# The LSTM's input products of two steps as seven block products, with partial sums taken out of PSUM by VectorE

## The chip, the cores and the metric

The kernel runs on one core of one Trainium2 chip. The metric is the device time of one execution in microseconds (us). The kernel before takes 1242.64 us, the median of three runs (1242.17 to 1243.83).

## The reference: what is computed

An LSTM over 128 time steps and then a GRU over the same 128 steps, for 32 sequences, with 512 features and a state of 512. Each layer's output is added to its input.

```python
# LSTM (Wx, Wh: 512 x 2048), h0 = cond_1024, c0 = 0
a = x[:, t] @ Wx + b + prev_h @ Wh
i, f, o = sigmoid(a[:, :512]), sigmoid(a[:, 512:1024]), sigmoid(a[:, 1024:1536])
g = tanh(a[:, 1536:])
c = f * c + i * g ;  h = o * tanh(c)
y = x + h                                   # input of the GRU
# GRU (each of W*, U*: 512 x 512), its state s starts at 0; video = cond_1024
z  = sigmoid(y[:, t] @ W_z + s @ U_z + vz)  # vz = video @ C_z + b_z, and so on
r  = sigmoid(y[:, t] @ W_r + s @ U_r + vr)
hh = tanh(y[:, t] @ W + (r * s) @ U + vh)
s  = (1 - z) * s + z * hh
out = y + s
```

## The kernel before

**Tiles.** The four chunks of 32 columns of a gate lie on four groups of 32 partitions. So every product is issued as four matmuls, one for each j, each with a stationary operand of 128 x 32 (32 sequences of one chunk of 128 features) and a moving one of weights; the four write four partition groups of one PSUM bank and run beside each other. I call four such matmuls a set.

**Precision.** Each fp32 operand is split into a high and a low fp16 part, and a product is three passes: high by high, high by low, low by high (PASSES). With four chunks of features (K) that is 12 sets for a product over all features. The scales of the split come from the largest |x| of a group of four steps (largest, bound, lstm_scales, gru_scales). The first steps (t < FL = 4 for the LSTM, t < F = 8 for the GRU) use fp32 matmuls on the weights as given, while the weights are split.

**A tick.** `ticks` runs t from 0 to 128. In tick t the LSTM does step t and the GRU step s = t - 1. Each engine has its own program, in order, and semaphores join them; the order is written by hand. q = t % 4 is the place in the group, r the half of the double buffers. On TensorE a tick from t = 9 on is:

- the product of `wh` with the LSTM's state, 512 columns, 12 sets (waits `h_hi`, `h_lo`), in bank `ps_l[t % 4]`; with it the gates of step t are complete
- the product of `w` with y, 384 columns (three gates), 12 sets (waits `y_hi`, `y_lo`, and `cand_sum`), in `ps_g`
- the product of `u` with the GRU's state, 256 columns (z and r), 12 sets (waits `g_hi`, `g_lo`); `zr_ps` tells VectorE
- the product of `wx` with x of step t + 1, 512 columns, 12 sets, in bank `ps_l[(t+1) % 4]` (waits `ifo_sum` of three steps ago); once in each group `bound` follows
- the product of `u` with r * s, 128 columns, 12 sets (waits `rg_hi`, `rg_lo`); `cand_ps` tells VectorE

**VectorE in a tick:** the gates' sums out of PSUM (`undone`: times a scale, plus a bias), `ig_fc`, the cell, the sum for z and r, then the new state (`new_state`), `rg`, its transpose and its parts, the low part of h, `keep`, the work of the group (`turn`, `lstm_scales`, `turn_out`, the low part of x, `gru_scales`, `largest`), the candidate's sum, `zc`, `g_nat`, its transpose and its low part. ScalarE does the sigmoids, tanhs and the high parts; GpSimd (POOL) adds x and h into yT, scales it, makes the low part of y, and adds up the output. SP issues the loads of x and the stores.

**Lines.** L780 is the matmul of `product`, L541 is `undone`, L538 `lo_part`, L346 ScalarE's `hi_part`, L889 the wait ahead of the product with `w`, L928 the wait for `x_lo` ahead of the product with `wx`, L822 `bound`.

Of the kernel before, what the change touches and what calls it, by code (L numbers as in the profile page):

```python
# [5 lines left out]
def lstm_then_gru(nc, x, cond, wx, wh, b0, w_z, u_z, c_z, b_z, w_r, u_r, c_r, b_r, w_h, u_h, c_h, b_h, out):  # L6
# [8 lines left out]
    B, T, D = x.shape  # L15
# [34 lines left out]
    with ExitStack() as ctx:  # L50
# [75 lines left out]
        ps_c = psum("ps_c", [P, GL * P])  # L126
        ps_squares = ps_c[:, GG * P:GG * P + 2 * K + 2 * GG]
# [23 lines left out]
        cond_ps = sem("cond_ps")  # L151

# [81 lines left out]

        @block.sync
        def _(sp):
# [28 lines left out]
            def tick(t, n, i):  # L265
                q, r = n % Q, n // Q
                group = 2 * i + r
                if q == 0 and (group + 2 < NG):

                    sp.wait_ge(xT_done, group + 1)  # L270
                    load(t + 2 * Q, r)
                if t >= 2 * Q + 1 and t % Q == (1 if t < T else 0):
                    store(Q * (group - 2), r, group - 2)
# [7 lines left out]
        def _(pool):  # L281
# [24 lines left out]
            def tick(t, n, i):  # L306
# [28 lines left out]
        def _(act):  # L335
# [107 lines left out]
            def tick(t, n, i):  # L443
# [25 lines left out]
                if (q == 1 and 0 < group < NG - 1) or t == 2:  # L469
# [16 lines left out]
                after_cand(t)  # L486

# [3 lines left out]
        def _(dve):  # L491
# [51 lines left out]
            def lstm_scales(r, group):  # L543
# [4 lines left out]
                nc.vector.tensor_scalar(t0, ps_bound[:, r:r + 1], 1.0, None, ALU.add).then_inc(base_done, 1)  # L548
# [72 lines left out]
            def after_keep(t):  # L621
# [12 lines left out]
                if t == T_WU_SCALE + 4:  # L634
                    u_low(1, 1)

            def after_cand(t):
# [39 lines left out]
            def tick(t, n, i):  # L677
# [7 lines left out]
                if lstm:  # L685
                    if q == 0:
                        dve.wait_ge(scl_done, group + 1)
                    dve.wait_ge(gates_ps, t + 1)
                    undone(gates[:, 3 * P:4 * P], ps_l[t % NL][:, 3 * P:4 * P], r_l(r), term0[:, 3, :]).then_inc(tg_sum, 1)
                    undone(ifo, ps_l[t % NL][:, 0:3 * P], r_l(r), term0[:, 0:3, :].rearrange("p g c -> p (g c)")  # L690
                           ).then_inc(ifo_sum, 1)
# [41 lines left out]
                if q == 0 and 0 < group < NG - 1:  # L733
# [4 lines left out]
                if t >= 2 * Q + 1 and t % Q == (1 if t < T else 0):  # L738
                    dve.wait_ge(out_done[r], 16 * J * i)
                    turn_out(r, group - 2)  # L740
                if q == 2 and (group + 1 < NG):
                    dve.wait_ge(x_hi, group + 1)
                    lo_part(x2T[:, 1 - r, LO, :], xT[:, 1 - r, :], a_x(1 - r), x2T[:, 1 - r, HI, :]).then_inc(x_lo, 1)
# [3 lines left out]
                if q == 3 and (group + 2 < NG):  # L747
                    dve.wait_ge(x_in[r], 16 * J * (i + 2))
                    largest(r)
                if gru:  # L750
# [3 lines left out]
                    after_cand(t)  # L754
                    dve.wait_ge(cand_done, s + 1)
# [7 lines left out]
                    nc.vector.transpose(gT[:, s % 2, :], g_nat[:]).then_inc(gT_done, 1)  # L763
                    if F - 1 <= s < T - 1:
# [9 lines left out]
        def _(pe):  # L774
# [26 lines left out]
            def w_of(b, k, j):  # L801
                return w12[:, b, k, :, :].rearrange("p g (n j c) -> p j (g n) c", j=J, c=B)[:, j]
# [13 lines left out]
            HALF, WAIT = 6, 8  # L816
# [12 lines left out]
            def gate_as_given(bank, g, still, raw_weights, chunks, opens, closes):  # L829
# [3 lines left out]
                return mm  # L833

# [10 lines left out]
            def tick(t, n, i):  # L845
# [15 lines left out]
                elif lstm:  # L861
                    if t == FL:
                        pe.wait_ge(wh_split, HALVES * K)
                    pe.wait_ge(h_hi, t + 1 - FL)
# [21 lines left out]
                elif F <= m < T:  # L886
# [3 lines left out]
                    product(ps_g[m % 2], 0, GG * P, w_of, y_of(m % Q), 0, HALF, True, False)  # L890
# [31 lines left out]
                if FL - 1 <= t < T - 1:  # L922
# [7 lines left out]
                if q == 0 and 0 < group < NG - 1:  # L930
                    bound(1 - r, group + 1)
                if recurs and s < F:
# [40 lines left out]
```

## Time and profile before

| | |
|---|---|
| time, median of 3 runs | 1242.64 us (1242.17 to 1243.83) |
| the profiled execution's own time | 1244.18 us |
| its span | 1242.4 us |
| mean granted clock of TensorE | 0.989 of full speed |
| TensorE matmuls busy | 1205.5 us, 97% of the span |
| TensorE weight loads busy | 763.8 us, 61% |
| VectorE busy | 872.4 us, 70% |
| ScalarE busy | 445.0 us, 36% |
| GpSimd busy | 278.0 us, 22% |

PE is TensorE's matmuls and PEld its weight loads, which run beside them; DVE is VectorE, ACT ScalarE, POOL GpSimd. Times of the trace are counted from the start of the span. A row of matmuls shows when its first began and for how long the row ran; its end is modelled and overlaps the next row, so a block of sets is measured from its start to the start of the next.

### The profile page before, as it was taken

What the parts mean: (1) busy time and instruction counts of PE and PEld (TensorE: products, weight loads), DVE (VectorE), ACT (ScalarE), POOL (GpSimd) and SP (SyncE); (2) the same over time, 40 slices, a digit from 0 to 9 for tenths busy, and PEclk for the clock granted to TensorE, in tenths of its full rate; (3) what the DMA queues carried; (4) which work ended last, traced back from release to release, by engine and by line L of the source; (5) the groups of instructions that cost most, each with busy time, mean ns of one, the idle gap of its engine ahead of it and who ended that gap; (6) DMA issues with size and microseconds to landing.
All of it is one profiled execution on the core that took longest, in us unless ns stands there. A gap on an engine that the chain in (4) does not pass through costs nothing.

```text
span 1242.4 us, 67987 instructions
## 1 busy us (share of the span) xinstructions
PE 1205.5 (97%) x31013; PEld 763.8 (61%) x31013; DVE 872.4 (70%) x2681; ACT 445.0 (36%) x1078; POOL 278.0 (22%) x520
## 2 busy tenths in 40 slices
PE   5889999999999999999999999999999999999996
PEld 1457666666666666666666666666666666666664
DVE  2568877777777777777776777777777777677765
ACT  5555233333333333333333333333333333333332
POOL 3100222222212222222222221222222222222221
PEclk9899999999999999999999999999999999999998
DMA  9900100111110111110011111011111001110001
GB/s 304 317 9 12 20 10 14 21 20 20 21 19 6 20 21 21 20 21 12 12 21 21 20 21 20 5 19 20 21 21 21 13 11 21 20 20 12 12 8 24
DMA packets 142000, 39.50 MB, mean 32 GB/s; under 512 B 135760, under 2 KB 136016, under 8 KB 140688
## 3 DMA queue, kind: packets, MB, share of 16 engines
q1 hardware_dynamic: 140016, 34.49, 12.9%
q8 instruction: 243, 3.98, 1.3%
q0 software_dynamic: 640, 0.53, 0.2%
q14 instruction: 45, 0.37, 0.1%
q10 hardware_dynamic: 1056, 0.13, 0.1%
HBM read 26.74 MB, written 8.39 MB: 28 GB/s over the span
## 4 chain that ended last, share of the span: by engine, by line
PE 93%; SPq 3%; DVE 2%; DMA 1%; issue 1%; ACT 0%; POOLq 0%; POOL 0%; DVEq 0%
PE ps_l L780 51%; PE ps_g L780 38%; PE ps_g L789 3%; SPq L239 2%; DMA o_area<-in_L_cond_C_dram 1%; PE ps_l L789 1%; SPq L243 1%; PE ps_bound L822 0%; DVE wh L538 0%; DVE u L538 0%; DVE zr L541 0%; SPq L248 0%; SPq L250 0%; PE ps_c L789 0%; ACT zr L457 0%
## 5 line engine op out<-in xcount | busy, mean ns | idle before, releaser
L780 PE MATMUL ps_l<-wh,h2T 128*32 128x512 f16 x5952 | 344.4, 380 | 3.3 <-DVE wh L538 3.3
L780 PE MATMUL ps_l<-wx,x2T 128*32 128x512 f16 x5952 | 342.8, 379 | 0.0
L780 PE MATMUL ps_g<-w,y2T 128*32 128x384 f16 x5760 | 256.2, 327 | 0.0
L780 PEld LDWEIGHTS ps_l<-wx,x2T 128*32 128x32 f16 x5952 | 160.6, 97 | 134.2
L780 PEld LDWEIGHTS ps_l<-wh,h2T 128*32 128x32 f16 x5952 | 154.6, 97 | 138.7 <-DVE wh L538 3.6
L780 PEld LDWEIGHTS ps_g<-w,y2T 128*32 128x32 f16 x5760 | 155.3, 97 | 92.3
L320 POOL TENSOR_TENSOR yT<-xT,hT 128x128 f32<-128x128 f32 x128 | 61.9, 484 | 589.8 <-DVE hT L670 589.8
L780 PE MATMUL ps_g<-u,g2T 128*32 128x256 f16 x5760 | 178.5, 273 | 0.8 <-ACT g2T L485 0.8
L780 PEld LDWEIGHTS ps_g<-u,g2T 128*32 128x32 f16 x5760 | 154.7, 97 | 16.9 <-issue 1.2
L541 DVE SCALAR_TENSOR_TENSOR zr<-ps_g,sc,term 128x256 f32<-128x256 f32 x128 | 61.9, 484 | 108.0 <-PE ps_g L780 100.5
L304 POOL TENSOR_TENSOR o_area<-yT,gT 128x128 f32<-128x128 f32 x128 | 58.6, 458 | 307.3 <-DVE gT L763 307.3
L541 DVE SCALAR_TENSOR_TENSOR gates<-ps_l,sc,term 128x128 f32<-128x128 f32 (+1 forms) x256 | 111.4, 476 | 13.7 <-PE ps_l L789 6.3
L696 DVE TENSOR_TENSOR ig_fc<-gates,tg_cell 128x256 f32<-128x256 f32 x128 | 54.4, 425 | 76.5 <-ACT gates L450 76.4
L780 PE MATMUL ps_g<-u,rg2T 128*32 128x128 f16 x5760 | 101.9, 220 | 4.4 <-DVE rg2T L535 4.4
L780 PEld LDWEIGHTS ps_g<-u,rg2T 128*32 128x32 f16 x5760 | 90.2, 97 | 25.2 <-DVE rg2T L535 4.6
L457 ACT ACTIVATE zr<-zr 128x256 f32<-128x256 f32 x128 | 53.3, 416 | 134.8 <-DVE zr L541 134.7
L479 ACT ACTIVATE cand<-cand 128x128 f32<-128x128 f32 x128 | 39.6, 309 | 155.3 <-DVE cand L541 155.3
L485 ACT ACTIVATE g2T<-gT,sc 128x128 f16<-128x128 f32 x120 | 48.3, 402 | 125.9 <-DVE gT L763 125.9
L538 DVE SCALAR_TENSOR_TENSOR g2T<-gT,sc,g2T 128x128 f16<-128x128 f32 x120 | 42.1, 351 | 58.5 <-ACT g2T L485 58.5
L328 POOL TENSOR_TENSOR y2T<-y_scaled,y2T 128x128 f16<-128x128 f32 x120 | 68.7, 573 | 49.6 <-ACT y2T L468 49.6
L325 POOL TENSOR_SCALAR y_scaled<-yT,sc 128x128 f32<-128x128 f32 x120 | 77.1, 643 | 11.8
L448 ACT ACTIVATE tg_cell<-gates 128x128 f32<-128x128 f32 x128 | 39.6, 310 | 107.0 <-DVE gates L541 107.0
(101 smaller groups left out, 1107.3 us busy)
## 6 DMA issues: line engine op xcount, KB each, us to landing
out_dram<-o_area SPq DMA_DIRECT2D x128, 64.0 KB, 2.1
x_nat<-in_x_dram SPq DMA_DIRECT2D x126, 64.0 KB, 2.7
wh<-in_L_cond_Wx_dram SPq DMA_DIRECT2D x4, 1024.0 KB, 12.0
w<-in_L_cond_Wh_dram SPq DMA_DIRECT2D x3, 1024.0 KB, 20.4
u<-in_L_cond_Wh_dram SPq DMA_DIRECT2D x1, 1024.0 KB, 26.5
stage<-in_L_cond_W_z_dram SPq DMA_DIRECT2D x1, 1024.0 KB, 8.5
stage<-in_L_cond_W_r_dram SPq DMA_DIRECT2D x1, 1024.0 KB, 8.1
stage<-in_L_cond_W_dram SPq DMA_DIRECT2D x1, 1024.0 KB, 10.3
```

What stands on the lines that cost most here:

```text
L304: nc.gpsimd.tensor_tensor(oT[:, r, q, :], yT[:, q, :], gT[:, m % 2, :], ALU.add).then_inc(oT_done, 1)
L320: nc.gpsimd.tensor_tensor(yT[:, q, :], xT[:, r, P * q:P * q + P], hT[:, n % 2, :], ALU.add).then_inc(yT_done, 1)
L325: nc.gpsimd.tensor_scalar(y_scaled[:, n % 2, :], yT[:, q, :], a_y(r), None, ALU.mult).then_inc(y_scaled_done, 1)
L328: nc.gpsimd.tensor_tensor(y2T[:, q, LO, :], y_scaled[:, n % 2, :], y2T[:, q, HI, :], ALU.subtract).then_inc(y_lo, 1)
L448: nc.scalar.activation(tg_cell[:, 0:P], gates[:, 3 * P:4 * P], ACT.Tanh)
L457: nc.scalar.activation(zr[:], zr[:], ACT.Sigmoid).then_inc(zr_done, 1)
L485: nc.scalar.mul(g2T[:, HI, :], gT[:, s % 2, :], a_g(m_next // Q)).then_inc(g_hi, 1)
L538: return nc.vector.scalar_tensor_tensor(lo, value, scale, hi, ALU.mult, ALU.subtract)
L541: return nc.vector.scalar_tensor_tensor(to, ps, scale, term, ALU.mult, ALU.add)
L696: nc.vector.tensor_tensor(ig_fc[:], gates[:, 0:2 * P], tg_cell[:], ALU.mult).then_inc(ig_fc_done, 1)
L780: mm = nc.tensor.matmul(bank[B * j:B * j + B, c0:c1].rearrange("p (n c) -> p n c", c=B), still(a, k), moving(b, k, j), start=opens and (a, ...
L789: mm = nc.tensor.matmul(bank[rows(j), c0:c0 + weights.shape[1] // J].rearrange("p (n c) -> p n c", c=B), still[:, B * chunk:B * chunk + B] ...
```

## The change

For a pair of steps u, u + 1 (u even, u >= FW = 24) the input products are a product of a matrix of 2 by 2 blocks (two steps by two halves of the features) with one of 2 by 2 blocks (two halves of the features by two halves of the 2048 columns). They are made from seven products of blocks instead of eight, with sums of blocks of x (S1 to S4) and of blocks of Wx (T1 to T4). One block product is 6 sets (three passes, two chunks) of 256 columns. Four partial sums for each pair leave PSUM through VectorE into `pre`, in place of the bias, and the gates' sums then add `pre` instead of `term0`. The rest:

- Wx is loaded again at t = 9; GpSimd makes T1 to T4 at t = 11 to 14 (two subtractions of 128 x 1024 in each), ScalarE splits one at the end of ticks 12, 13, 15 and 16, VectorE makes the low parts in ticks 13, 14, 16 and 17, two instructions of 128 x 1024 in each. GpSimd makes S1 to S4 once for each group at q = 3 (128 x 128 each); they are split once for each group (128 x 512).
- From t = 9 on (m >= F) the product of `w` is in two: 256 columns (z and r) at its old place, and 128 columns (the candidate's) just before the product with r * s, behind a wait for `zr_sum`.
- The work of a group stands elsewhere: `turn_out` and the store at q = 3 of the next group; for groups from the sixth on `largest` at q = 2, `turn` at q = 3, the scales at q = 0 and x's parts at q = 0 and 1, most of them right behind the gates' sums on VectorE.

```diff
@@ VectorE
+            def first_out(u):
+                evict(1, u, pre[:, u % NL, H1], ps_l[(u + 1) % NL][:, H2], bias0(H1))
+            def fifth_out(u):
+                evict(2, u, pre[:, (u + 1) % NL, H2], ps_fifth[:, H1], bias0(H2))
+            def sixth_out(u):
+                dve.wait_ge(evicted, 2 * (u - FW) + 2)
+                evict(3, u, pre[:, u % NL, H2], ps_l[(u + 1) % NL][:, H2], pre[:, (u + 1) % NL, H2])
+            def seventh_out(u):
+                evict(4, u, pre[:, (u + 1) % NL, H1], ps_l[(u + 1) % NL][:, H2], bias0(H1))
...
+                if q == 0 and NG_W <= group + 1 < NG:
+                    lstm_scales(1 - r, group + 1)
...
+                if FW <= t < T and q % 2 == 0:
+                    seventh_out(t)
...
+                    if FW <= t + 2 < T and q % 2 == 0:
+                        first_out(t + 2)
+                    if FW <= t + 1 < T and q % 2 == 1:
+                        sixth_out(t + 1)
...
+                    if FW <= t + 2 < T and q % 2 == 0:
+                        fifth_out(t + 2)
@@ TensorE
+                    if t >= FW and q % 2 == 1:
+                        pe.wait_ge(evicted, 2 * (t - FW) + 2)
                     pe.wait_ge(h_hi, t + 1 - FL)
...
-                    product(ps_g[m % 2], 0, GG * P, w_of, y_of(m % Q), 0, HALF, True, False)
+                    product(ps_g[m % 2], 0, 2 * P, w_of(0, 2), y_of(m % Q), 0, WAIT, True, False)
+                    pe.wait_ge(y_lo, m + 1 - F)
+                    product(ps_g[m % 2], 0, 2 * P, w_of(0, 2), y_of(m % Q), WAIT, END, False, False)
...
-                if FL - 1 <= t < T - 1:
+                if FL - 1 <= t < FW - 1:
...
+                if q % 2 == 0:
+                    if FW <= t < T:
+                        pe.wait_ge(evicted, 2 * (t - FW) + 3)
+                        seventh(ps_l[(t + 1) % NL], 1, s_of(r, 3, q // 2), t_of(N_T3), False).then_inc(seven_ps, 1)
+                    if FW <= t + 2 < T:
...
+                        pe.wait_ge(ifo_sum, v - NL + 1)
+                        seventh(ps_l[v % NL], 0, a_of(ru, qu + 1, 1), t_of(N_T4), True)
+                        seventh(ps_l[v % NL], 1, a_of(ru, qu, 0), b_of(0, 0), False).then_inc(seven_ps, 1)
...
+                        seventh(ps_fifth, 0, s_of(ru, 1, qu // 2), t_of(N_T1), True).then_inc(seven_ps, 1)
+                elif FW <= t + 1 < T:
...
+                    pe.wait_ge(evicted, 2 * (u - FW) + 1)
+                    seventh(ps_l[v % NL], 1, s_of(ru, 2, qu // 2), t_of(N_T2), False).then_inc(seven_ps, 1)
+                    pe.wait_ge(ifo_sum, u - NL + 1)
+                    seventh(ps_l[u % NL], 0, a_of(ru, qu, 1), b_of(1, 0), True)
+                    seventh(ps_l[u % NL], 1, s_of(ru, 4, qu // 2), b_of(1, 1), False)
...
+                if F <= m < T:
+                    pe.wait_ge(zr_sum, m + 1)
+                    product(ps_g[m % 2], 2 * P, 3 * P, w_of(2, 3), y_of(m % Q), 0, END, False, False)
@@ GpSimd and ScalarE
+                if t == T_MADE:
+                    pool.wait_ge(again_in, 16 * K)
+                    make_t(t1, b12, b11)
...
+                if T_MADE + 1 <= t <= T_MADE + 2:
+                    split_high(t - T_MADE - 1)
```

TensorE, two ticks in the middle of the kernel before (`product` is L780; `x48` is 12 sets):

```order
L780 MATMUL ps_l<-wh,h2T 32x512 x48
L780 MATMUL ps_g<-w,y2T 32x384 x48
L780 MATMUL ps_g<-u,g2T 32x256 x48
L780 MATMUL ps_l<-wx,x2T 32x512 x48
L780 MATMUL ps_g<-u,rg2T 32x128 x48
L780 MATMUL ps_l<-wh,h2T 32x512 x48
L780 MATMUL ps_g<-w,y2T 32x384 x48
```

The same engine now, an even tick from its product with `u` on, and the odd one behind it (L963 is `product`, L1023 the block product `seventh`, `stage` holds the T, the S and `pre`, `ps_c` is the fifth partial sum's bank):

```order
L963 MATMUL ps_g<-u,g2T 32x256 x48
L1023 MATMUL ps_l<-stage 32x256 x24
L1023 MATMUL ps_l<-stage,x2T 32x256 x24
L1023 MATMUL ps_l<-wx,x2T 32x256 x24
L1023 MATMUL ps_c<-stage 32x256 x24
L963 MATMUL ps_g<-w,y2T 32x128 x48
L963 MATMUL ps_g<-u,rg2T 32x128 x48
L963 MATMUL ps_l<-wh,h2T 32x512 x48
L963 MATMUL ps_g<-w,y2T 32x256 x48
L963 MATMUL ps_g<-u,g2T 32x256 x48
L1023 MATMUL ps_l<-stage 32x256 x24
L1023 MATMUL ps_l<-wx,x2T 32x256 x24
```

(One more block product of the odd tick follows.) The product of `wx` with 512 columns became four block products in the even tick and three in the odd one, and the candidate's part of the product with `w` moved behind them.

VectorE in a tick with q = 2 of the kernel before, from the keep on:

```order
L730 SCALAR_TENSOR_TENSOR keep<-zr,g_nat 128x128
L538 SCALAR_TENSOR_TENSOR x2T<-xT,sc,x2T 128x512
L558 TENSOR_SCALAR sc<-factors,base 128x2
L559 TENSOR_SCALAR sc<-undo,base 128x1
L541 SCALAR_TENSOR_TENSOR cand<-ps_g,sc,term 128x128
L756 TENSOR_TENSOR zc<-zr,cand 128x128
L759 TENSOR_TENSOR g_nat<-zc,keep 128x128
L763 STREAM_TRANSPOSE gT<-g_nat 128x128
L538 SCALAR_TENSOR_TENSOR g2T<-gT,sc,g2T 128x128
```

The same stretch now (L654 is `undone`, L651 `lo_part`):

```order
L900 SCALAR_TENSOR_TENSOR keep<-zr,g_nat 128x128
L654 SCALAR_TENSOR_TENSOR stage<-ps_l,sc,term 128x256
L675 TENSOR_SCALAR sc<-factors,base 128x2
L676 TENSOR_SCALAR sc<-undo,base 128x1
L654 SCALAR_TENSOR_TENSOR cand<-ps_g,sc,term 128x128
L654 SCALAR_TENSOR_TENSOR stage<-ps_l,sc,term 128x256
L937 TENSOR_TENSOR zc<-zr,cand 128x128
L940 TENSOR_TENSOR g_nat<-zc,keep 128x128
L944 STREAM_TRANSPOSE gT<-g_nat 128x128
L654 SCALAR_TENSOR_TENSOR stage<-ps_c,sc,term 128x256
L651 SCALAR_TENSOR_TENSOR g2T<-gT,sc,g2T 128x128
```

Three partial sums stand in an even tick: ahead of the candidate's sum, behind it, and behind the transpose of g. The odd tick has one, behind the candidate's sum. The low part of x moved to the front of the tick before.

## Rows read from the trace of the kernel before

**Rows 1.** Busy us (x instructions) of PE, PEld, DVE, ACT, POOL; PEclk; DMA.

```profile
300.00:400.00 100.00, 100.00 (x2631) 63.47 (x2627) 71.85 (x227) 33.33 (x89) 23.54 (x44) 1.00 0.08 14
1200.00:1243.00 43.00, 31.32 (x824) 20.57 (x811) 23.80 (x71) 9.95 (x27) 6.92 (x15) 0.86 0.13 21
```

**Rows 2.** Timeline, one tick: start us, us, engine, line, op.

```profile
600.92 2.76 PE L780 MATMUL ps_l<-wx,x2T 128*32 128x512 f16 x48
601.15 0.48 DVE L541 SCALAR_TENSOR_TENSOR zr<-ps_g,sc,term 128x256 f32<-128x256 f32 x1 [0.69 <-PE ps_g L780]
...
603.12 0.35 DVE L538 SCALAR_TENSOR_TENSOR rg2T<-rgT,sc,rg2T 128x128 f16<-128x128 f32 x1
...
603.51 0.84 PE L780 MATMUL ps_g<-u,rg2T 128*32 128x128 f16 x48
...
603.85 0.68 DVE L562 TENSOR_REDUCE raw<-x_nat 128x1 bf16<-128x512 f32 x1
603.88 0.43 POOL L328 TENSOR_TENSOR y2T<-y_scaled,y2T 128x128 f16<-128x128 f32 x1 [0.41 <-ACT y2T L468]
...
604.18 2.76 PE L780 MATMUL ps_l<-wh,h2T 128*32 128x512 f16 x48
604.44 0.34 DVE L541 SCALAR_TENSOR_TENSOR cand<-ps_g,sc,term 128x128 f32<-128x128 f32 x1
...
605.16 0.29 DVE L756 TENSOR_TENSOR zc<-zr,cand 128x128 f32<-128x128 f32 x1 [0.38 <-ACT cand L479]
...
606.16 0.40 ACT L485 ACTIVATE g2T<-gT,sc 128x128 f16<-128x128 f32 x1 [1.03 <-DVE gT L763]
...
606.60 0.35 DVE L538 SCALAR_TENSOR_TENSOR g2T<-gT,sc,g2T 128x128 f16<-128x128 f32 x1 [0.47 <-ACT g2T L485]
606.77 2.12 PE L780 MATMUL ps_g<-w,y2T 128*32 128x384 f16 x48
607.06 0.88 DVE L541 SCALAR_TENSOR_TENSOR gates<-ps_l,sc,term 128x128 f32<-128x128 f32 x2
...
608.53 0.42 DVE L696 TENSOR_TENSOR ig_fc<-gates,tg_cell 128x256 f32<-128x256 f32 x1 [0.59 <-ACT gates L450]
...
608.72 1.48 PE L780 MATMUL ps_g<-u,g2T 128*32 128x256 f16 x48
...
610.03 2.76 PE L780 MATMUL ps_l<-wx,x2T 128*32 128x512 f16 x48
```

**Rows 3.** Groups by shape, 300 to 1200 us: busy us, mean ns, idle before.

```profile
L541 DVE SCALAR_TENSOR_TENSOR zr<-ps_g,sc,term 128x256 f32<-128x256 f32 x98 | 47.4, 484 | 80.7 <-PE ps_g L780 80.7
L304 POOL TENSOR_TENSOR o_area<-yT,gT 128x128 f32<-128x128 f32 x98 | 44.9, 458 | 203.7 <-DVE gT L763 203.7
L538 DVE SCALAR_TENSOR_TENSOR x2T<-xT,sc,x2T 128x512 f16<-128x512 f32 x25 | 18.6, 745 | 0.0
L474 ACT ACTIVATE x2T<-xT,sc 128x512 f16<-128x512 f32 x24 | 17.2, 718 | 0.0
```

**Rows 4.** Groups by shape, 90 to 180 us, where W and U are split.

```profile
L538 DVE SCALAR_TENSOR_TENSOR w<-stage,cols,w 128x1024 f16<-128x1024 f32 x6 | 7.5, 1278 | 0.0
L346 ACT ACTIVATE u<-stage,cols 128x2048 f16<-128x2048 f32 x3 | 5.9, 1988 | 0.0
```

**Rows 5.** Timeline of PE around the last tick of that split.

```profile
140.88 1.49 PE L780 MATMUL ps_g<-u,g2T 128*32 128x256 f16 x48 [0.83 <-ACT g2T L485]
...
145.32 0.85 PE L780 MATMUL ps_g<-u,rg2T 128*32 128x128 f16 x48 [0.36 <-DVE rg2T L535]
```

**Rows 6.** Line L928, then L889: waits of PE's sequencer, first and last start.

```profile
L928 PEldq EVENT_SEMAPHORE  x1: 51/51/51, 600.2 to 600.2; - x1
L889 PEldq EVENT_SEMAPHORE  x1: 51/51/51, 605.3 to 605.3; - x1
```

**Rows 7.** Timeline of PE at the end.

```profile
1226.98 3.48 PE L780 MATMUL ps_g<-w,y2T 128*32 128x384 f16 x48
```

**Rows 8.** The page's DMA issues: KB each, median us to landing.

```profile
wh<-in_L_cond_Wx_dram SPq DMA_DIRECT2D x4, 1024.0 KB, 12.0
```

More of the change, by code:

```diff
@@ L151, in lstm_then_gru @@
         cond_ps = sem("cond_ps")
+        again_in = sem("again_in")
+        t_made = sem("t_made")
+        t_hi = sem("t_hi")
+        t_split = sem("t_split")
+        xs_done = sem("xs_done")
+        xs_hi = sem("xs_hi")
+        xs_lo = sem("xs_lo")
+        seven_ps = sem("seven_ps")
+        evicted = sem("evicted")
         raw_x = sem("raw_x")
@@ L271, in tick @@
                     load(t + 2 * Q, r)
-                if t >= 2 * Q + 1 and t % Q == (1 if t < T else 0):
-                    store(Q * (group - 2), r, group - 2)
+                if t == T_AGAIN:
+                    sp.wait_ge(cand_ps, F - 1)
+                    sp.wait_ge(w1_split, HALVES * GG)
+                    sp.wait_ge(u1_split, HALVES * GG)
+                    for k in range(K):
+                        sp.dma_start(wx_again[k], wx[P * k:P * k + P, :]).then_inc(again_in, 16)
+                if q == Q - 1 and group >= 1:
+                    store(Q * (group - 1), 1 - r, group - 1)
             ticks(tick)
@@ L296, in _ @@
                 pool.sem_inc(out_done[r], 16 * J)
+            pool_made = [0]
             def add_out(s, m, group):
@@ L468, in tick @@
                     nc.scalar.copy(y2T[:, q, HI, :], y_scaled[:, n % 2, :]).then_inc(y_hi, 1)
-                if (q == 1 and 0 < group < NG - 1) or t == 2:
+                if (q == 1 and 0 < group < NG_W - 1) or t == 2:
                     act.wait_ge(xT_done, group + 2)
@@ L732, in tick @@
                 after_keep(t)
-                if q == 0 and 0 < group < NG - 1:
+                if FW <= t < T and q % 2 == 0:
+                    seventh_out(t)
+                if q == 0 and 0 < group < NG_W - 1:
                     if t >= Q:
@@ L746, in tick @@
                         gru_scales(1 - r, group + 1)
-                if q == 3 and (group + 2 < NG):
+                if q == 3 and group + 2 < NG_W:
                     dve.wait_ge(x_in[r], 16 * J * (i + 2))
@@ L833, in gate_as_given, with seventh, a_of, s_of @@
                 return mm
+            def seventh(bank, half, operand, weights, opens):
+                for a, b in PASSES:
+                    for k in range(K // 2):
+                        for j in range(J):
+                            mm = nc.tensor.matmul(bank[rows(j), 2 * P * half:2 * P * half + 2 * P].rearrange("p (n c) -> p n c", c=B),
+                                                  operand(a, k),
+                                                  weights(b, k).rearrange("p (n j c) -> p j n c", j=J, c=B)[:, j],
+                                                  start=opens and (a, b, k) == (HI, HI, 0), stop=(a, b, k) == (LO, HI, K // 2 - 1),
+                                                  skip_group_check=True)
+                return mm
+            def a_of(r, q, half):
+                return lambda a, k: x2T[:, r, a, P * q + B * (2 * half + k):P * q + B * (2 * half + k) + B]
+            def s_of(r, n, m):
+                c = P * (n - 1) + P // 2 * m
+                return lambda a, k: xs2[:, r, a, c + B * k:c + B * k + B]
+            def b_of(half, columns):
+                return lambda b, k: wx2[:, b, 2 * half + k, N2 * columns:N2 * columns + N2]
+            def t_of(n):
+                return lambda b, k: t_parts[n][:, b, k, :]
             pe.wait_ge(zeroed, 3)
```

145 lines of the change are left out of this document (128 added, 17 removed).

## The prediction

> **What bounds the kernel now.** I read the busy time by stretch first [rows 1]. From 300 to 400 us, as in each stretch to 1200, TensorE is busy for 100.00 of 100 us at clock 1.00, VectorE for 72, ScalarE for 33, GpSimd for 24. Busy matmuls can still be stretched ones, so next I read the timeline of one tick by the starts of its blocks [rows 2]: `wx` 600.92 to 603.51 is 2.59 us for 12 sets of 512 columns, `u` with r * s to 604.18 is 0.67 (128 columns), `wh` to 606.77 is 2.59, `w` to 608.72 is 1.95 (384), `u` to 610.03 is 1.31 (256). The sum is 9.11 us, the next `wx` starts 9.11 us after the first, and no row of PE has an idle time. Per set this is 216, 56, 162 and 109 ns: each is its columns at 2.4 GHz (213, 53, 160, 107) and about 2.5 ns more. So TensorE's columns set the time. `bound` comes once in a group before and after, so it drops out.
>
> **TensorE's sum.** Before, a pair of ticks has two `wx` blocks, 5.18 us. Now it has seven block products of 6 sets of 256 columns, at the `u` block's 1.31 us for 12 sets: 7 x 0.655 = 4.585. That is 0.595 less. The product of `w` is now 1.31 + 0.67 = 1.98 instead of 1.95: 0.03 more in each tick. A pair gives back 0.595 - 0.06 = 0.535 us, and there are (128 - 24) / 2 = 52 pairs: **-27.8 us**. The 16 ticks from 9 to 24 and the last pay only the 0.03: **+0.5 us**.
>
> **Do the states still come in time?** I set Z as the start of the block behind `u`. The sum for z and r starts at Z + 0.23 and then VectorE runs without a pause to Z + 2.93, where `keep` has made room (603.85 less 600.92) [rows 2]. Now r * s goes in at Z + 2.62 + 0.67 = Z + 3.29 in an even tick and Z + 1.97 + 0.67 = Z + 2.64 in an odd one. Its high part is ready when its low part starts, Z + 2.20, its low part 0.35 later, needed 0.45 us into the block: 0.4 us to spare in the odd tick, over 1 in the even one. `wh` starts at Z + 3.96 or Z + 3.31.
>
> The four evictions have the shape of the sum for z and r, 484 ns, some 0.43 of VectorE's time each [rows 3]. They stand in its idle times. The seventh goes from Z + 2.93 to about Z + 3.4; the candidate's sum must wait for TensorE until about Z + 4.15 anyway, and `wh` of the odd tick, which waits for this eviction, starts at Z + 3.96: 0.5 us to spare. The first and the sixth lie between the candidate's sum and `zc`, which starts 0.72 us behind it because it waits 0.38 for ScalarE [rows 2]; 0.28 + 0.43 fill that exactly. The fifth lies before the low part of g, where VectorE waits 0.47. So g is ready 2.1 (high) to 2.5 us (low) behind the start of the candidate's sum, at Z + 6.3 and Z + 6.7, and `u` now asks for the high part 3.9 us behind the start of `wh`, at Z + 7.9 (even) or Z + 7.2 (odd, where the candidate's sum is 0.5 earlier too). Behind the gates' sums VectorE waits 0.59 for ScalarE; the 0.7 us moved there (the low part of x is 0.745) delays `ig_fc` by 0.1 to 0.3, and the sum for z and r starts 2.5 us behind the gates' sums, where `ig_fc` and the cell were done at 2.2. ScalarE has 1.4 us more at the end of the q = 0 tick (twice 0.718), 0.5 of it past the start of the next gates' tanh; that uses the 0.3 up and no more. y has 2.7 us before `w` asks for it (603.88 + 0.43 against 606.77 less the GpSimd's semaphore), and the four sums S take 4 x 0.458 in a queue that idles for three quarters. Cost of all this at steady state: **0**. If VectorE's cover were gone the price would be the overrun in each tick.
>
> **The T blocks, ticks 12 to 17.** VectorE gets two instructions of 1.28 us in each of four ticks, ScalarE one of 1.99 at the end of four [rows 4]. Followed: ScalarE ends its split 0.9 us late for tick 13's tanh, 1.8 late for tick 14's; r * s is late by some 0.5 there. In tick 14 VectorE has 2.56 and x's low part and scales ahead of g: g's high part about 1.5 late for `u`. Tick 16 (the turn of x and its scales) 1.3 late, tick 17 0.9 and 0.3. Sum 4.5 us. The same working for tick 8 of the kernel before, with three such instructions, gave 1.2 us where the row says 0.83 [rows 5], so I take it for a little high, and its range from 2 to 8: **+4.5 us**. Tick 9's two waits of before, 0.83 and 0.36: the first grows by the missing 0.65 and the 128 columns then cover the second: **+0.1**.
>
> GpSimd's subtractions of 128 x 1024 are not in the trace. From the nearest row, 458 ns for 128 columns [rows 3], they take 0.46 us (all of it fixed) to 3.7 (all by column). At 3.7 two in a tick and its own 2.1 us are 9.5 in a tick of 9.1, four times: 1.6 us late, against y's 2.7. I cost them at 0 at both ends; a slower rate than the row's would show in y. Wx again is four loads of 12.0 us each [rows 8], issued together when U is split, about when tick 9's `u` block starts (140.88) [rows 5], and wanted late in tick 11, over 20 us later: in time if they overlap as at the start.
>
> **The end.** At 1226.98 the clock has fallen (0.86 in the last stretch; the last `w` block's row is 3.48 us long, 2.12 in mid-kernel) [rows 1, 2, 7]. `w` of 256 columns is 0.65 shorter in tick 127 and about 1 in tick 128, and the candidate's columns run while TensorE waits for r * s: **-1.6 us**.
>
> **Sum** against the profiled execution (1244.18 us, span 1242.4): -27.8 + 0.5 + 4.5 + 0.1 - 1.6 = -24.3, so 1219.9. That execution is 1.5 above the median of the runs; from 1242.64 it gives 1218.3. I say **1219**.
>
> **Can TensorE be fed that fast?** A pair had 480 matmuls, each with its load, in 18.2 us: 38 ns for each of the two together. Now it has 648 in 17.7: 27 ns, and the 96 ahead of every `wh` run at 14. The trace shows how far the sequencer is ahead: it met the wait at L928 at 600.2, 0.7 us before the block behind it began at 600.92, and L889 at 605.3, 1.5 before 606.77 [rows 6]. At 27 and at 54 ns for a matmul both are some 26 matmuls, also behind 24 matmuls at 27 ns, so a pace of 27 does not drain it. The block of r * s took 48 in 0.67 us and `wh` followed without a gap: with 26 in store the supply is at most 26 ns for each. Now 96 and the first 4 behind them need 74 beyond the store in 1.34 us, 18 ns each. The rows allow anything from 0 to 26, and the cost goes from nothing up to 74 x 26 - 1340, near 0.6 us a tick, 70 us over 120 ticks. I take 0, since the nearest row (the block at 14 ns for each) shows no stretch at all.
>
> The Trainium skill has a rule against this change: "Runtime: NRT & Kernel Launch", section "Instruction fetch mechanics", names a floor of about 20 cycles for each instruction. The page's floor, as an estimate at the 1.2 GHz of the sequencer in "Advanced Engine Details and Errata", section "Clock Domains", is 33 ns for a matmul with its load, and the changed kernel would then be slower by some 1.9 us a tick. The trace disagrees: 48 matmuls with their loads at 27 ns each in the `u` block left the sequencer as far ahead as before [rows 2, 6].
>
> **Rivals.**
>
> 1. *The feeding binds* (the other side). Place: the 96 matmuls of 128 columns. It costs from 18 ns up, and cancels the gain of 24 us at 0.2 us a tick, a supply of 20.8 ns. At the middle of what then remains, 23.5 ns: 74 x 23.5 - 1340 = 0.40 us, 120 times 48: **1267 us**. For it: nothing in the trace ran 96 in a row at this pace. Against: the block of 48 is exact to the last set.
> 2. *VectorE becomes a part of the bound.* It gets 4 x 0.43 and a quarter of 0.745 twice for each pair, so from 6.6 us a tick to some 7.6 of 8.84, and each eviction fits by 0.1 or less in its idle time. If each tick lost 0.15 (reads of PSUM beside TensorE's writes, longer waits): 104 x 0.15 = 16: **1235 us**.
> 3. *The T phase is costlier*, VectorE, ScalarE and GpSimd pushing each other beyond the 8: +8 more, **1227 us**.
> 4. *The seven products don't run at the `u` block's pace* (their moving operand lies in `stage` and is read with another stride). At 5 ns more for a set, 42 x 5 = 0.2 us a pair: **1230 us**.
>
> **Chances.** The forecast 0.58 (its own range 1214 to 1224), rival 1 0.14, rival 2 0.13, rival 3 0.08, rival 4 0.07. The range leaves the upper part of rival 1 out and keeps the best case, no stall at T and the full sum: 1214 to 1245. 0.2% is 2.5 us, about what a measurement of this kernel can tell from no change. Faster than 1240.2: 0.58, nearly all of 2, 3 and 4, a little of 1: 0.83. Within: 0.05. Slower: 0.12.
>
> **What will show it.** In a tick after 220 us block products of 0.655 us from start to start and no idle row of PE; a pair of 17.7 us; `w` of 128 columns directly ahead of r * s, both at 0.67. Rival 1 shows as 12 sets of 128 columns that take more than 0.67 while every semaphore has long been there. Rival 2 shows as PE rows with an idle time from `evicted`, `rg2T` or `g2T`. The T phase shows PE idle between 170 and 220 us: 2 to 8 us in all. The prediction is wrong if PE idles at all in steady ticks, or if the pair is not 17.7.

## The result

The changed kernel takes 1309.44 us, the median of four runs (1307.51 to 1313.48), against 1242.45 for the kernel before beside it. The ratio is 1.054, with a 95% interval from 1.051 to 1.057: 67 us slower, where the forecast was 23 faster. TensorE's clock is no large part of that: the granted clock is 0.99 on the mean in both profiled executions, and 1.00 in mid-kernel. Between the start and the end of the kernel it falls only where T is made, as told below.

The stretches of the changed kernel, as [rows 1] of before (busy us of PE, PEld, DVE, ACT, POOL with the number of instructions; PEclk; DMA share; GB/s):

```profile
180.00:220.00 40.00, 31.08 (x868) 19.73 (x860) 33.68 (x68) 14.21 (x30) 21.24 (x18) 0.91 0.10 16
300.00:400.00 100.00, 94.64 (x3422) 81.77 (x3411) 79.62 (x240) 34.64 (x90) 26.79 (x51) 1.00 0.09 15
```

TensorE, which had no idle time in [rows 1], has 5 us in each 100 of the steady part, and 9 in the 40 around the making of T. The waits between 300 and 1200 us say what ended them (us in total, times, longest us):

```profile
PE ps_g L963 <- issue: 30.8, 39, 1.5
PE ps_l L963 <- issue: 14.7, 23, 1.3
PE ps_l L963 <- DVE stage L654: 2.7, 2, 1.5
PE ps_l L1023 <- issue: 1.0, 4, 0.3
```

"Issue" is time in which TensorE waited for no semaphore. The evictions (`stage L654`) end two of the waits. The timeline shows where such a stop stands, here over an even tick:

```profile
608.54 0.92 PE L1023 MATMUL ps_l<-stage 128*32 128x256 f16 x24
...
609.20 0.92 PE L1023 MATMUL ps_l<-stage,x2T 128*32 128x256 f16 x24
...
609.86 0.50 PE L1023 MATMUL ps_l<-wx,x2T 128*32 128x256 f16 x11
...
610.69 0.61 PE L1023 MATMUL ps_l<-wx,x2T 128*32 128x256 f16 x13 [0.34 <-issue]
...
611.04 0.93 PE L1023 MATMUL ps_c<-stage 128*32 128x256 f16 x24
...
611.69 0.88 PE L963 MATMUL ps_g<-w,y2T 128*32 128x128 f16 x47
...
612.42 0.77 PE L963 MATMUL ps_g<-u,rg2T 128*32 128x128 f16 x40
614.71 0.11 PEld L963 LDWEIGHTS ps_g<-u,rg2T 128*32 128x32 f16 x5 [1.70 <-issue]
614.71 0.29 PE L963 MATMUL ps_g<-u,rg2T 128*32 128x128 f16 x5 [1.52 <-issue]
614.81 2.31 PEld L963 LDWEIGHTS ps_l<-wh,h2T 128*32 128x32 f16 x48
614.84 2.77 PE L963 MATMUL ps_l<-wh,h2T 128*32 128x512 f16 x48
```

While it runs, a block product keeps its pace: 608.54 to 609.20 is 0.66 us. But work stops in the middle of a block, after 11 of 24 or after some 43 of 48 matmuls, with nothing to wait for, and weight loads stop with it. Between the stops stand:

```profile
602.45:610.65 8.20, 7.86 (x256) 6.38 (x255) 6.44 (x22) 2.67 (x7) 3.02 (x8) 1.00 0.28 44
610.65:614.65 4.00, 2.49 (x128) 2.30 (x128) 1.34 (x5) 0.30 (x1) 0.95 (x2) 1.00 0.01 4
```

Matmuls and loads together, 512 and then 256. I took all pauses over 260 ns between two starts of TensorE from 300 to 1200 us: 80, and each of the 79 distances between them is a multiple of 256 instructions within 4. The DMA queue that brings instructions agrees in its packets. Its row of the changed kernel (packets, MB, share of 16 engines' span):

```profile
q8 instruction: 317, 5.19, 1.7%
```

Before it had 243 packets, so 74 more; TensorE has 40517 - 31013 = 9504 matmuls and as many loads more, and 19008 / 256 = 74.3. So I call 256 instructions a page.

The packets of this queue, taken one by one from the trace, also show what ends the stops. Each has 16 KB and takes 1.0 us. In the even tick above one runs from 608.40 to 609.35 us and TensorE goes on at 610.69; the next runs from 612.28 to 613.16 and TensorE goes on at 614.71. In all 80 pauses TensorE goes on 1.2 to 1.6 us behind the end of such a packet, while an instant taken at random lies anywhere from 0 to 4.4 us behind one; and the next packet starts 1.1 to 2.1 us, 1.2 in the median, after TensorE has gone on. So at a stop the turn is 1.0 us for the packet, 1.4 until TensorE runs, and 1.2 until the next packet: 3.6 us for 256 instructions. What fills the 1.4 and the 1.2 is not shown. The packets from 300 to 1200 us are 3.81 us apart on the mean (3.24 at the least).

The Trainium skill says the same of the size of a page ("Runtime: NRT & Kernel Launch", section "Instruction fetch mechanics": blocks of 256 instructions, fetched while the block before runs); it also calls the fetch hidden, which this trace contradicts.

**Where the 67 us come from.** I follow the start of the `wh` block. Before it is at 274.21 us in tick 24 and at 1218.12 in tick 127. Now:

```profile
294.76 2.58 PE L963 MATMUL ps_l<-wh,h2T 128*32 128x512 f16 x44
...
1289.71 1.48 PE L963 MATMUL ps_l<-wh,h2T 128*32 128x512 f16 x24 [0.40 <-DVE stage L654]
```

The 103 ticks take 994.95 us instead of 943.91: 51 us more, where 27 less were forecast. This execution took 1313.48 us, 4 above the median, and the forecast for it was 1219.9; the 78 us are the larger part of these 94. The rest lies before tick 24, which begins 20.6 us late: 15 of them from ticks 12 to 17 (forecast: 4.5), 2.2 from a stop in tick 10, and 2.0 from tick 22, which already does three block products of the first pair and is no loss. The end gave back 2.4 us, where 1.6 were forecast.

Of the 15 us, some 3 are the clock. It falls twice, each time behind a wait for g's parts, and there the blocks behind the wait take longer (start to start: `wx` 3.71 us instead of 2.59, `u` 2.54 instead of 1.31):

```profile
194.95 1.06 PE L963 MATMUL ps_g<-u,g2T 128*32 128x256 f16 x32 [2.09 <-ACT g2T L584]
...
197.37 3.88 PE L963 MATMUL ps_l<-wx,x2T 128*32 128x512 f16 x48
201.08 0.84 PE L963 MATMUL ps_g<-w,y2T 128*32 128x128 f16 x48
...
210.34 2.75 PE L963 MATMUL ps_g<-u,g2T 128*32 128x256 f16 x48 [3.85 <-ACT g2T L584]
212.88 2.97 PE L963 MATMUL ps_l<-wx,x2T 128*32 128x512 f16 x48
```

The granted clock is 0.83 of full speed from 190 to 200 us and 0.84 from 210 to 220, so for a part of each it is at the lower of its two levels, 1.2 GHz; the kernel before has 1.00 there.

### The profile page after: what moved, and what is told of

Same layout as the page of the kernel before. It is cut to its first block, busy times and chain, and to the rows that moved or that the text cites. A ratio compares the mean times of both kernels' runs of the same rounds, so it can differ in the third digit from the quotient of the medians.

```text
span 1311.6 us, 87594 instructions
## 1 busy us (share of the span) xinstructions
PE 1206.6 (92%) x40517; PEld 980.3 (75%) x40517; DVE 1000.3 (76%) x2923; ACT 465.0 (35%) x1108; POOL 348.3 (27%) x632
## 4 chain that ended last, share of the span: by engine, by line
PE 84%; issue 6%; DVE 5%; SPq 3%; DMA 1%; ACT 1%; POOLq 0%; POOL 0%; DVEq 0%
PE ps_g L963 36%; PE ps_l L963 26%; PE ps_l L1023 16%; PE ps_g L972 3%; PE ps_c L1023 3%; SPq L289 2%; DMA o_area<-in_L_cond_C_dram 1%; SPq L293 1%; PE ps_l L972 1%; DVE g_nat L940 1%; DVE stage L651 0%; ACT stage L441 0%; DVE zc L937 0%; DVE zr L654 0%; DVE cand L654 0%
## 5 line engine op out<-in xcount | busy, mean ns | idle before, releaser
L963 PE MATMUL ps_l<-wh,h2T 128*32 128x512 f16 x5952 | 358.2, 381 | 24.2 <-issue 17.6
L963 PE MATMUL ps_g<-w,y2T 128*32 128x128 f16 (+1 forms) x11520 | 296.0, 246 | 4.7 <-issue 3.4
L963 PEld LDWEIGHTS ps_l<-wh,h2T 128*32 128x32 f16 x5952 | 180.5, 97 | 148.4 <-issue 35.7
L963 PEld LDWEIGHTS ps_g<-w,y2T 128*32 128x32 f16 x11520 | 260.9, 97 | 30.6 <-issue 5.9
L963 PE MATMUL ps_g<-u,g2T 128*32 128x256 f16 x5760 | 187.8, 274 | 12.3 <-ACT g2T L584 11.7
L963 PEld LDWEIGHTS ps_g<-u,g2T 128*32 128x32 f16 x5760 | 163.4, 97 | 16.2 <-ACT g2T L584 12.2
L963 PE MATMUL ps_g<-u,rg2T 128*32 128x128 f16 x5760 | 113.0, 219 | 34.6 <-issue 31.8
L963 PEld LDWEIGHTS ps_g<-u,rg2T 128*32 128x32 f16 x5760 | 91.1, 97 | 41.8 <-issue 38.2
L654 DVE SCALAR_TENSOR_TENSOR gates<-ps_l,sc,stage 128x128 f32<-128x128 f32 x208 | 91.1, 479 | 33.7 <-PE ps_l L963 30.4
L654 DVE SCALAR_TENSOR_TENSOR cand<-ps_g,sc,term 128x128 f32<-128x128 f32 x128 | 44.6, 349 | 90.3 <-PE ps_g L963 88.7
L654 DVE SCALAR_TENSOR_TENSOR zr<-ps_g,sc,term 128x256 f32<-128x256 f32 x128 | 61.9, 483 | 50.3 <-PE ps_g L963 42.9
L1023 PE MATMUL ps_l<-wx,x2T 128*32 128x256 f16 x2496 | 94.2, 273 | 1.1 <-issue 1.0
L1023 PE MATMUL ps_l<-stage 128*32 128x256 f16 x2496 | 94.2, 273 | 0.0
L551 ACT ACTIVATE tanh_c<-tg_cell 128x128 f32<-128x128 f32 x128 | 39.7, 310 | 108.7 <-DVE tg_cell L868 108.7
```

Of the source, the lines that this page charges most:

```text
L551: nc.scalar.activation(tanh_c[:], cell, ACT.Tanh).then_inc(tanh_c_done, 1)
L654: return nc.vector.scalar_tensor_tensor(to, ps, scale, term, ALU.mult, ALU.add)
L963: mm = nc.tensor.matmul(bank[B * j:B * j + B, c0:c1].rearrange("p (n c) -> p n c", c=B), still(a, k), moving(b, k, j), start=opens and (a, ...
L1023: mm = nc.tensor.matmul(bank[rows(j), 2 * P * half:2 * P * half + 2 * P].rearrange("p (n c) -> p n c", c=B), operand(a, k), weights(b, k). ...
```

## The experiments

Theory P: instructions reach TensorE in pages of 256, a page costs at least some 3.8 us, and the sequencer's lead covers little of that. The changed kernel has 648 instructions a tick (matmuls and their loads), 2.53 pages: 9.6 us, against 8.84 of columns. Before had 480, 1.88 pages: 7.1 us, hidden under 9.11. R is the rate that I had as a rival: a fixed time for each matmul with its load. V: the evictions and the waits around them.

**halves.** Only the number of instructions, without any of the change:

```diff
+                cuts = [(c0, c1)] if c1 - c0 < GL * P else [(0, 2 * P), (2 * P, 4 * P)]
                 for a, b, k in steps[first:last]:
+                  for c, d in cuts:
                     for j in range(J):
...
```

> The kernel before, with each product of 512 columns (wh and wx) issued as two of 256: the same columns, 336 matmuls in a tick instead of 240, no seven products, no evictions, no new wait. Theory P (instructions reach TensorE in pages of 256, and a page costs at least some 3.8 us): 672 instructions are 2.63 pages, 9.97 us a tick instead of 9.11, about +100 us, 1345 us, with idle times of PE at every 256th instruction. Rival R (each matmul with its load costs the dispatch 18 to 26 ns, no more): a pace of 27 ns is within it, only the 2.5 ns of each set more, +7 us, 1250. Rival V (the evictions and waits of the seven products cost the time): +7 us, 1250.

Measured: 1334.68 us, ratio 1.073 (1.071 to 1.075): 91 us more, near P's 100 and far from the 7 of R and V. TensorE stops in the middle of blocks (timeline):

```profile
606.00 2.56 PE L782 MATMUL ps_l<-wh,h2T 128*32 128x256 f16 x85
608.89 0.51 PE L782 MATMUL ps_l<-wh,h2T 128*32 128x256 f16 x11 [0.33 <-issue]
609.13 2.22 PE L782 MATMUL ps_g<-w,y2T 128*32 128x384 f16 x48
```

From 300 to 1200 us there are 98 such pauses, all 97 distances between them are multiples of 256 within 4, and each ends 1.2 to 1.7 us behind a packet of the instruction queue. A tick is 9.87 us without `bound`; over 672 / 256 pages that is 3.76 us for each, and the changed kernel's own 9.60 over 2.53 gives 3.79. P holds, R and V fall: no eviction is in this kernel, and its pace of 27 ns a matmul is that of the `u` block of before.

**split_w.** Of the change, only the product of w in two parts:

```diff
-                    product(ps_g[m % 2], 0, GG * P, w_of, y_of(m % Q), 0, HALF, True, False)
+                    product(ps_g[m % 2], 0, 2 * P, w_of(0, 2), y_of(m % Q), 0, WAIT, True, False)
...
+                    pe.wait_ge(zr_sum, m + 1)
+                    product(ps_g[m % 2], 2 * P, 3 * P, w_of(2, 3), y_of(m % Q), 0, END, False, False)
```

> The kernel before, with only the product of w in two parts, 256 columns at its place and 128 directly ahead of the product with r * s (96 matmuls of 128 columns in a row). P: 576 instructions a tick are 2.25 pages, 8.55 us against 9.14, the dense stretch is covered by the slow ones beside it: +3.6 us, 1246, at most 1250. R: the 96 in a row need 18 ns each and lose 0.3 to 0.6 us in each of 120 ticks: +40 to +70 us. V: +4 us.

Measured: 1245.18 us, ratio 1.0015 (1.0005 to 1.0025). The 96 matmuls of 128 columns run without a stop:

```profile
603.53 0.84 PE L780 MATMUL ps_g<-w,y2T 128*32 128x128 f16 x48
604.20 0.84 PE L780 MATMUL ps_g<-u,rg2T 128*32 128x128 f16 x48
604.87 2.76 PE L780 MATMUL ps_l<-wh,h2T 128*32 128x512 f16 x48
```

So the dense stretch that I had named as the place of the rival costs nothing by itself. It matters only with few slow instructions beside it: 576 a tick are 4.06 us a page, over 3.8. A single page's worth may be well under 3.8: the densest 256 instructions of this kernel start within 2.87 us (4.13 in the kernel before), the densest 512 within 7.22, and TensorE doesn't stop. So 3.8 us is a limit on the mean over more than one page.

**no_evict.** The changed kernel with `first_out`, `fifth_out`, `sixth_out` and `seventh_out` not called and the waits on `evicted` gone.

> The changed kernel without its four evictions and all waits on them; the gates' sums add the bias alone, so those partial sums are left out of the result. TensorE's program is the same. P: as the changed kernel, 1305 to 1312 us. R: the same. V: the steady ticks go to 8.84 us, some 1225 to 1235.

Measured: 1300.12 us, ratio 1.0455 (1.0434 to 1.0476). Nine us of 67 are VectorE's evictions or their waits; V is no explanation of the rest. TensorE still stops, and the instruction packets are 3.76 us apart on the mean, as in halves (3.77); the evictions had made that 3.81.

**whole_w.** The changed kernel with w whole:

```diff
-                    product(ps_g[m % 2], 0, 2 * P, w_of(0, 2), y_of(m % Q), 0, WAIT, True, False)
+                    product(ps_g[m % 2], 0, GG * P, w_of(0, GG), y_of(m % Q), 0, WAIT, True, False)
...
-                    product(ps_g[m % 2], 2 * P, 3 * P, w_of(2, 3), y_of(m % Q), 0, END, False, False)
```

> The changed kernel with the product of w whole again (384 columns) at its old place: 552 instructions a tick instead of 648. P: 2.16 pages are 8.2 us, under the 8.81 of the columns; the odd tick waits 0.25 us for r * s, so about 8.95 a tick and 1235 to 1242 us. R: the 96 in a row are gone too, the same 1235 to 1242. V: -3 us, 1306.

Measured: 1250.79 us, ratio 1.0058 (1.0043 to 1.0073). One edit gives back 59 us. The time is 9 us above the range I gave. No stop for issue is left on a matmul between 300 and 1200 us; what is left there is late data. (This run doesn't tell P from R, which forecast the same; halves and split_w do.) Timeline of an odd tick and the even tick behind it:

```profile
707.84 0.83 PE L1023 MATMUL ps_l<-wx,stage 128*32 128x256 f16 x24
708.82 0.85 PE L963 MATMUL ps_g<-u,rg2T 128*32 128x128 f16 x48
709.50 2.76 PE L963 MATMUL ps_l<-wh,h2T 128*32 128x512 f16 x48
...
717.97 0.84 PE L963 MATMUL ps_g<-u,rg2T 128*32 128x128 f16 x48
718.81 2.77 PE L963 MATMUL ps_l<-wh,h2T 128*32 128x512 f16 x48
```

r * s comes 0.33 us late behind three block products (0.98 us from 707.84, not 0.65), and `wh` of the odd tick 0.17 late (0.84 from 717.97, not 0.67): the seventh eviction.

**whole_w_early** gives TensorE two sets of wh ahead of r * s in odd ticks:

```diff
+                    pe.wait_ge(h_hi, t + 2 - FL)
+                    product(ps_l[u % NL], 0, GL * P, wh_of, state_of(h2T), 0, EARLY, False, False)
```

> The changed kernel with w whole and, in odd ticks, the first 2 of the 12 sets of the next step's product with wh ahead of the product with r * s, so that the latter finds its operand ready. P: no stop for pages, 8.82 us a tick and 0.06 for bound, against 9.17: some 103 x 0.3 = 30 us less than before, and 17 to 20 us more for the T phase: 1228 to 1233 us. R: the same. V: as the changed kernel, above 1290.

Measured: 1241.48 us, ratio 0.9985 (0.9975 to 0.9994). The wait for r * s is gone (9 us); the one for the eviction I had left out of the sum, so 8 us of the miss are that.

**pool_subs.** To see the T phase by itself, its eight GpSimd subtractions in the kernel before:

```diff
+                if 11 <= t <= 14:
+                    for c in (0, SLAB // 2):
+                        c = slice(c, c + SLAB // 2)
+                        nc.gpsimd.tensor_tensor(stage[:, t - 11, c], stage[:, 4, c], stage[:, 5, c], ALU.subtract)
```

> The kernel before with eight subtractions of 128 x 1024 added to GpSimd, two each behind its own work in ticks 11 to 14 (into memory that nothing reads any more). Theory S (a GpSimd instruction with two SBUF inputs and a VectorE instruction with two SBUF inputs keep each other waiting until the one is done): zc and g_nat grow from 0.29 us to 1 to 2.4, g2T comes 1 to 2 us late for u in each of the four ticks: +4 to +8 us. Rival D (only the low parts of T on VectorE and ScalarE's splits cost the T phase): less than 1 us, TensorE not idle in those ticks.

Measured: 1250.95 us, ratio 1.0066 (1.0049 to 1.0083), 8 us. Timeline of POOL and of VectorE in tick 11:

```profile
162.89 4.76 POOL L337 TENSOR_TENSOR stage<-stage 128x1024 f32<-128x1024 f32 x2
```

```profile
163.79 1.63 DVE L764 TENSOR_TENSOR zc<-zr,cand 128x128 f32<-128x128 f32 x1 [0.38 <-ACT cand L487]
165.45 2.35 DVE L767 TENSOR_TENSOR g_nat<-zc,keep 128x128 f32<-128x128 f32 x1
167.84 0.31 DVE L771 STREAM_TRANSPOSE gT<-g_nat 128x128 f32<-128x128 f32 x1
```

zc, 0.29 us in [rows 2], takes 1.63, g_nat 2.35, and each ends 0.15 us behind the end of a subtraction of 2.4 us. `cand`, which reads one of its inputs from PSUM, keeps its 0.34 us beside the first (163.07). The changed kernel shows the same (g_nat 2.35 us at 168.18).

**pool_ones.** The same with one input: `tensor_scalar(..., stage[:, 4, c], 0.5, None, ALU.mult)`.

> As pool_subs, with each subtraction replaced by a multiplication by a constant of the same 128 x 1024 (one SBUF input instead of two). Theory S (two inputs on both sides collide): zc and g_nat keep 0.29 us, 0 to +1 us in all. If any long GpSimd instruction holds VectorE's two-input ones: they wait for its whole length, +1 to +4 us.

Measured: 1243.54 us, ratio 1.0002 (0.9992 to 1.0011). The instructions are longer, and VectorE doesn't notice (POOL, then VectorE, same tick):

```profile
163.09 5.51 POOL L337 TENSOR_SCALAR stage<-stage 128x1024 f32<-128x1024 f32 x2
```

```profile
163.97 0.30 DVE L764 TENSOR_TENSOR zc<-zr,cand 128x128 f32<-128x128 f32 x1 [0.38 <-ACT cand L487]
164.30 0.29 DVE L767 TENSOR_TENSOR g_nat<-zc,keep 128x128 f32<-128x128 f32 x1
```

So two inputs on both engines collide, not length. The Trainium skill ("GPSIMD Engine Reference", section "Key points") names contention with VectorE instructions that have two SBUF inputs; the section doesn't tell one input of GpSimd's from two, and here only two collide. I had not counted it. It goes the other way too: in the changed kernel the low part of y on GpSimd takes 1.45 us instead of 0.43 when it starts beside a low part of T on VectorE (128 x 1024, 1.28 us, at 188.82).

**reload.** The kernel before with the four loads of Wx at t = 9.

> The kernel before with only Wx loaded again (4 MB) at t = 9. If the load delays the fetch of TensorE's instructions, as the stop of 1 us in tick 10 of the changed kernel suggests: TensorE idle for issue between 140 and 160 us, +0.5 to +2 us. If not: no idle time there.

Measured in one run: 1245.02 us. The load runs from 141.3 to 154.1 us. There are two stops of the weight loads for issue in the window, but the matmuls keep their pace: `wh` starts at 146.74, `w` at 149.33, 2.59 us apart. The expected loss isn't there. But the page's packet does come late: it starts 8.98 us behind the one before it (138.31, 147.29), where the kernel before has 6.06 at the same place.

**split_reload.** The same load beside the split product of w.

> The kernel before with w in two parts and with Wx loaded again at t = 9. Each alone left TensorE's ticks 9 to 11 as they were. P: the load makes the fetch of a page longer, and with 576 instructions a tick (4.06 us a page) there is no room for it: 1 to 3 us of idle time for issue in ticks 10 and 11, as in the changed kernel (2.2 us). If the stop in tick 10 there was something else: none.

Measured in one run: 1247.70 us, with these stops (timeline of PE):

```profile
145.62 1.89 PE L787 MATMUL ps_l<-wh,h2T 128*32 128x512 f16 x29
148.43 1.26 PE L787 MATMUL ps_l<-wh,h2T 128*32 128x512 f16 x19 [0.92 <-issue]
...
153.35 2.13 PE L787 MATMUL ps_l<-wx,x2T 128*32 128x512 f16 x36 [0.39 <-issue]
...
157.08 0.24 PE L787 MATMUL ps_g<-u,rg2T 128*32 128x128 f16 x4 [0.32 <-issue]
```

Neither part alone stops TensorE's matmuls, both together do, as P would have it if a large load makes a page dearer. The instruction queue's packets show how: the load runs from 140.0 to 153.0 us, and the packet that is due in it starts 8.87 us behind the one before (137.35, 146.22), 5.93 in split_w. The packet itself takes 0.99 us, no more than without the load, and TensorE goes on at 148.43, 1.2 us behind its end. So the load makes the packet start late, not run longer; why it starts late is not shown. With one run of each, the 2.4 us that tick 10 loses are read from the traces, not from the times.

**spread_t.** whole_w_early with the T phase spread:

```diff
-                if t == T_MADE:
-                    make_t(t1, b12, b11)
+                if T_MADE <= t < T_MADE + 8:
+                    n_t, k_t = divmod(t - T_MADE, 2)
+                    make_t(*[(t1, b12, b11), (t3, b22, b12), (t2, b22, t1), (t4, b21, t2)][n_t], k_t)
```

> As the run before (whole w, two early sets), with the making of T1 to T4 spread: one subtraction of GpSimd in each of ticks 11 to 18 instead of two in ticks 11 to 14, one low part in a tick instead of two, the seven products from t = 28 on. Theory S: the T phase costs 2 to 6 us instead of 14 to 18, so 1217 to 1224 us, faster than the kernel before. If T costs by VectorE's and ScalarE's own work alone: 1222 to 1228.

Measured: 1236.49 us, ratio 0.9950 (0.9936 to 0.9965). Right in direction, and 12 us above the range of theory S. Ticks with one subtraction and nothing else (t = 11, 12) cost 0.1 at most, those with a subtraction and a low part, or behind a whole split on ScalarE, 0.6 to 2.5. The granted clock stays at 1.00 here.

**best.** So subtractions, half splits and low parts in different ticks, FW = 32, and the seventh eviction ahead of the low part of h:

```diff
+                if FW <= t < T and q % 2 == 0:
+                    seventh_out(t)
                 if FL - 1 <= t < T - 1:
```

> From the run spread_t: GpSimd's subtractions, ScalarE's halves of a split (128 x 1024 each, one a tick) and VectorE's low parts in different ticks (T1 and T3 at t = 11 to 18, T2 and T4 at 19 to 26), the seven products from t = 32 on, and the seventh eviction ahead of the low part of h. P with S: the steady even tick loses its 0.17 us of waiting (8.7 and 8.48 us), the T phase costs 2 to 5 us instead of 13: 1218 to 1224 us. If the T phase's cost doesn't come from the subtractions and splits meeting in a tick: 1226 to 1230.

Measured: 1220.78 us, ratio 0.9823 (0.9801 to 0.9844): 1.8% faster than the kernel before, and within the range. Several things changed at once, so the run shows that they suffice, not what each is worth. Ticks 12 to 28, with the making of T, cost 4.9 us. Waits of PE from 100 to 300 us, and a stretch of the steady part:

```profile
PE ps_g L952 <- DVE rg2T L641: 2.4, 7, 0.4
PE ps_g L952 <- ACT g2T L579: 1.2, 2, 0.8
```

```profile
300.00:400.00 100.00, 100.00 (x2915) 70.95 (x2911) 82.24 (x248) 34.72 (x93) 29.85 (x57) 1.00 0.12 20
```

TensorE is busy throughout again with VectorE at 82 to 86%. A pair of ticks without `bound` is 17.6 us (8.48 and 9.14), the columns of seven products with w whole.

## Why the prediction was wrong

- *What bounds the kernel, TensorE's sum.* The columns were counted rightly: the blocks run at 0.655 and 0.67 us, and best reaches the sum of its own blocks. The gain of seven products for eight is real, 0.3 us a tick: a pair takes 17.6 us in best, 18.2 before. What I set at zero was the cost of their instructions.
- *"Can TensorE be fed that fast?"* This is the step that failed. The term that "I take 0" put at nothing had a size of 0.76 us a tick, some 78 us in all. Some 9 of them are the evictions (no_evict); what is left is about the 70 that I had named as the worst end. And the mechanism was another one than rival 1's. I looked for a rate for each matmul and for the densest 96; split_w shows that these cost nothing. The limit is on the mean time of a page of 256, and my sentence that a pace of 27 ns "does not drain" the sequencer rested on blocks of 48 to 96 instructions, shorter than a page, in a kernel whose pages took 4.9 us (9.11 over 1.88). The rows had a warning: 648 instructions in 8.84 us are 3.5 us for 256, and the densest 256 of the kernel before take 4.13 (from the `u` block through `wx` to r * s, [rows 2]). No row said how much faster they could come.
- *The Trainium skill's floor of 20 cycles an instruction* ("Runtime: NRT & Kernel Launch", section "Instruction fetch mechanics"; 16.7 ns, as an estimate at the 1.2 GHz that the prediction cites) does not hold here: split_w runs 192 instructions at 7 ns each, and its whole tick at 15.9 ns each (9.14 us for 576). For the changed kernel the floor gives 10.8 us a tick; 9.60 was measured and 8.84 forecast. It had the direction right, and a page in 3.8 us, 14.8 ns for each instruction, is near it; but the mechanism is another one. I put it aside with an argument from a block of 96 instructions, which could not show a limit on 256.
- *The states in time.* Nearly right: r * s in odd ticks is needed at Z + 2.64 with w split and was in time; with w whole it is 0.33 late. The evictions' idle times held, but "0.5 us to spare" for the seventh went with the 0.67 that the split w had put ahead; and no_evict is 9 us faster, which I had at 0 (rival 2 in small: 0.05 us more for each page, 3.81 against 3.76; whether by late data or by the time VectorE takes is not separated).
- *The T phase.* Forecast 4.5 (2 to 8), measured 15. The terms left out are the collision of two-input instructions, 8 us by pool_subs, and the fall of the clock behind the long waits, some 3 us. With the 4.5 of the forecast they add up to the 15, but the three sizes come from different kernels, so that they add is not shown. I priced GpSimd's subtractions rightly (2.4 us, within 0.46 to 3.7) but asked only what waits behind them on GpSimd's own queue.
- *Wx again* came in time, but its load made a page of the denser instructions late: 2.2 us.
- *Rivals 3 and 4.* 3 happened, and larger (15 us, where its 8 on top of the 4.5 make 12.5), with a cause that it didn't name; 4 did not (0.655 us a block product from `stage` as from `wx`).

## What to carry to other kernels

Before an edit that trades columns for instructions, count TensorE's instructions, loads included, and work out the mean time of 256 over a whole tick of the new kernel (here 3.5 us). Compare it with what the chip has been seen to deliver (here 3.8); a floor on it does not show in a kernel that stays above it, and one dense stretch proves nothing either way (2.87 us for 256 in split_w, no stop). Halving a matmul's columns is not free even where the weight loads are hidden. And when work is moved to an idle engine, ask which operands it shares a path with: a long GpSimd instruction with two inputs belongs where VectorE has none to run.

## What the runs showed of the hardware

- TensorE's instructions come in pages of 256, one packet of 16 KB each, and where they bind a page takes 3.8 us on the mean (3.76 in halves, 3.79 in the changed kernel; the shortest distance between two packets is 3.24). A stop ends 1.2 to 1.7 us behind the end of a packet. Ticks of 4.06 us a page (split_w: 576 instructions in 9.14) show no stop of the matmuls, nor do those of whole_w (552 instructions in about 9.0 us, 4.2 a page).
- A load of 4 MB made the packet in it start some 3 us late (8.87 us behind the one before instead of 5.93); the packet still took 1.0 us.
- Within a page, 96 matmuls of 128 columns with their loads go at 14 ns each.
- A GpSimd subtraction of 128 x 1024 fp32 takes 2.4 us and holds a VectorE tensor_tensor with two SBUF inputs until it ends; a multiplication by a constant takes 2.8 us and holds nothing.
